# Causal mask of the query maxima added by VectorE, strip by strip, and the batches written out one by one

## What is computed

```python
def _L0_attn_ref(x, Wq, Wk, Wv, Wo):
    def proj(W):                       # 16 heads, 32 values each (real and imaginary part)
        return (x @ W).reshape(B, N, H, 2 * hd).transpose(0, 2, 1, 3)
    ...
    scores = (einsum(q_r, k_r) + einsum(q_i, k_i)) / sqrt(hd)
    scores = where(tril(ones((N, N))), scores, -inf)
    probs = softmax(scores, axis=-1)
    ...
    return out @ Wo
x = x + _L0_attn_ref(_layernorm(x), Wq, Wk, Wv, Wo)
x = x + _L0_xattn_ref(_layernorm(x), ctx, ctx)
x = x + _L0_ffn_ref(_layernorm(x), kernel, bias, a, b)
```

## Time and profile before

| | us |
|---|---|
| median of 3 runs | 828.6 (827.96 to 828.76) |
| the profiled execution | 827.51 |
| its span, first to last instruction | 825.7 |

### The profile page before, as it was taken

The page is one execution under the profiler, slowest core; times in us unless marked ns, Lnnn a source line. Parts: engine busy times, 40 slices in busy tenths (PEclk is TensorE's granted clock), DMA queues, the critical chain, the costliest instruction groups (busy, mean ns, idle before and its releaser), DMA issues.

```text
span 825.7 us, 15873 instructions
## 1 busy us (share of the span) xinstructions
PE 760.1 (92%) x5563; PEld 522.5 (63%) x5563; DVE 630.2 (76%) x1251; ACT 402.8 (49%) x760; POOL 472.1 (57%) x428
## 2 busy tenths in 40 slices
PE   3688999999999999999999999999999998989997
PEld 2565655765566556666666666565766564578995
DVE  2554555457769897999879997999788988798873
ACT  5114555555555466545645563647464546541111
POOL 5000000031966789677858786878677788975541
PEclk9759999999999999999999999999999998999997
DMA  5886656866686668566656675667466760101001
GB/s 180 111 105 83 98 78 85 135 83 85 84 135 78 90 85 135 74 89 108 90 101 89 103 93 100 89 104 96 71 95 109 95 88 8 58 14 36 5 13 38
DMA packets 47979, 70.53 MB, mean 85 GB/s; under 512 B 4897, under 2 KB 22578, under 8 KB 47922
## 3 DMA queue, kind: packets, MB, share of 16 engines
q1 hardware_dynamic: 46898, 69.52, 56.1%
q10 hardware_dynamic: 1024, 0.26, 0.1%
HBM read 14.98 MB, written 4.19 MB: 23 GB/s over the span
## 4 chain that ended last, share of the span: by engine, by line
PE 61%; DVE 15%; DMA 15%; issue 4%; ACT 2%; POOL 1%; SPq 1%; DVEq 0%; ACTq 0%; POOLq 0%
PE misc L521 21%; PE exp_bank L521 15%; DMA stack_k<-k_lo 14%; PE acc_bank L521 10%; PE max_bank L521 10%; PE sum_bank L521 3%; DVE neg_max L1205 3%; DVE score_rows L1217 2%; DVE head_out L1217 2%; SPq L452 1%; DVE seg_max L1205 1%; DVE ln_raw L1183 1%; PE misc L565 1%; ACT max_row L883 1%; PE misc L632 1%
## 5 line engine op out<-in xcount | busy, mean ns | idle before, releaser
L930 ACT ACTIVATE probs<-exp_bank 128x512 f32<-128x512 f32 x320 | 188.4, 592 | 203.7 <-PE exp_bank L521 200.9
L1205 DVE TENSOR_REDUCE neg_max<-max_bank 128x1 f32<-128x512 f32 (+1 forms) x192 | 130.3, 683 | 92.0 <-PE max_bank L521 91.5
L1580 POOL TENSOR_TENSOR prod<-head_probs,ctx_sb 128x256 f32<-128x256 f32 (+1 forms) x100 | 185.0, 1882 | 2.2 <-POOL head_probs L1575 0.5
L521 PE MATMUL max_bank<-stack_k,stack_q 96*128 96x384 f32 (+3 forms) x512 | 158.2, 372 | 17.1 <-DMA stack_k<-k_lo 8.7
L521 PE MATMUL acc_bank<-probs,values 128*32 128x512 f32 (+3 forms) x1024 | 158.6, 447 | 4.3 <-ACT log_sum L941 2.3
L314 POOL TENSOR_TENSOR prod<-x1n,ctx_sb 128x256 f32<-128x256 f32 (+1 forms) x104 | 158.7, 1557 | 4.3 <-ACT x1n L890 4.3
L521 PE MATMUL sum_bank<-probs,ones 128*32 128x512 f32 (+3 forms) x1024 | 157.8, 444 | 0.0
L521 PE MATMUL exp_bank<-stack_q,stack_k 97*128 97x384 f32 (+3 forms) x512 | 149.9, 355 | 1.8 <-DVE wf_lo L1175 1.3
L521 PEld LDWEIGHTS exp_bank<-stack_q,stack_k 97*128 97x128 f32 x512 | 84.5, 195 | 56.8 <-issue 26.5
L1520 POOL TENSOR_TENSOR ln_var<-ln_mv,eps 128x4 f32<-128x4 f32 x21 | 4.4, 210 | 197.8 <-DVE ln_mv L1191 197.8
L1205 DVE TENSOR_REDUCE seg_max<-max_bank 128x4 f32<-128x512 f32 x128 | 87.1, 683 | 29.2 <-PE max_bank L521 27.7
(11 more groups left out here) (181 smaller groups left out, 1381.8 us busy)
## 6 DMA issues: line engine op xcount, KB each, us to landing
stack_q<-q_hi SPq DMA_DIRECT2D x64, 256.0 KB, 5.6
stack_k<-k_hi SPq DMA_DIRECT2D x64, 256.0 KB, 9.5
stack_q<-q_lo SPq DMA_DIRECT2D x32, 256.0 KB, 7.0
stack_k<-k_lo SPq DMA_DIRECT2D x32, 256.0 KB, 10.7
x_in<-in_x SPq DMA_DIRECT2D x9, 512.0 KB, 5.5
ctx_sb<-in_ctx SPq DMA_DIRECT2D x32, 128.0 KB, 3.2
x<-in_x SPq DMA_DIRECT2D x7, 512.0 KB, 10.1
out<-y_sb SPq DMA_DIRECT2D x5, 512.0 KB, 3.3
```

Source lines behind the costliest of these rows:

```text
L521: return nc.tensor.matmul(*args, **kw)
L930: nc.scalar.activation(probs[:, (UNITS * g + n) % PTR, :], exp_bank[n % 2][:, :], ACT.Exp, scale=SCALE).then_inc(exp_done, 1)
L1205: vec.tensor_reduce(o, v, axis=AX_X, op=ALU.max, negate=True).then_inc(max_taken, 1)
L1580: last = gp.tensor_tensor(pv_prod[:, COFF[j]:COFF[j + 1]].rearrange("p (q d k) -> p q d k", q=4, k=keys), head_probs[:, 4 * j:4 * j + 4, N ...
```

## The change

It removes the mask matmul of every query unit, the tiles `mask_q`, `seg_max` and `neg_max`, the semaphore `max_ready` and the two small instructions behind the tenth unit. `take_max` issues one `tensor_tensor_reduce` per block instead, 16 per group in place of 10 reduces: it adds the right-hand end of `causal` (bf16, 512 columns, zero but for the last 128) to the block in place in PSUM, and keeps the maximum. Each of these is two instructions on DVE, the sum and a read of the accumulator, both shown as `ISA`. Its wait carries a wait on `const_ready` (long past) ahead. PE turns the maxima when `max_taken` has counted all ten units, and ACT negates them as it copies. The key side keeps its mask. The loop over batches is gone: all batches are written out.

```diff
     def batches(self, eng, body, n_batch):
-        first, after = 3, n_batch - 2
-        for i in range(-1, first):
-            body(i, i)
...
-        for i in range(after, n_batch):
+        for i in range(-1, n_batch):
             body(i, i)
...
-            def scores(bank, unit, lhs, rhs, slot, rows, key_side, done):
+            def query_scores(bank, unit, slot):
+
+                for h, blk, at, width in unit[0]:
+                    last = mm(bank[:, at:at + width], stack_q[0:STACK, slot, h, blk * P:(blk + 1) * P],
+                              stack_k[0:STACK, slot, h, 0:width], start=True, stop=True, skip_group_check=True)
+                last.then_inc(max_scored, 1)
...
             def turn_maxima(slot):
-                pe.wait_ge(max_ready, n_max_ready.up())
+                pe.wait_ge(max_taken, n_max_ready.up(UNITS))
...
-                            copy(max_row[:, m_slot % 2, :], misc[0][0:G * NT, 0:P]).then_inc(max_row_ready, 1)
+                            nc.scalar.activation(max_row[:, m_slot % 2, :], misc[0][0:G * NT, 0:P], ACT.Identity,
+                                                 scale=-1.0).then_inc(max_row_ready, 1)
...
             def take_max(n, ring):
 
-                dve.wait_ge(max_scored, n_scored.up())
+                wait_apart(dve, const_ready, (max_scored, n_scored.up()))
                 bank = max_bank[n % 2]
-                if n < G:
-                    o, v = neg_max[:, ring, n:n + 1, 3], bank[:, :]
-                elif n < 2 * G:
-                    o, v = seg_max[:, n - G, :], bank[:, :].rearrange("p (s k) -> p s k", k=P)
-                else:
-                    h = 2 * (n - 2 * G)
-                    o, v = neg_max[:, ring, h:h + 2, 1], bank[:, :].rearrange("p (s k) -> p s k", k=2 * P)
-                vec.tensor_reduce(o, v, axis=AX_X, op=ALU.max, negate=True).then_inc(max_taken, 1)
+                for h, blk, at, width in QUERY_UNITS[n][0]:
+                    v = bank[:, at:at + width]
+                    last = vec.tensor_tensor_reduce(v, v, causal[:, T - width:T], 1.0, -3.0e38, ALU.add, ALU.max,
+                                                    query_max[:, ring, h, blk:blk + 1])
+                last.then_inc(max_taken, 1)
...
-                            if unit == UNITS - 1:
-
-                                dve.wait_ge(max_taken, n_scored.now())
-                                vec.tensor_reduce(neg_max[:, ring, :, 2], seg_max[:, :, 0:3], axis=AX_X, op=ALU.min)
-                                vec.tensor_copy(neg_max[:, ring, :, 0], seg_max[:, :, 3]).then_inc(max_ready, 1)
```

More of the change, by code:

```diff
@@ L233, in decoder_layer @@
         stacked, max_stacked = sem("stacked"), sem("max_stacked")
-        max_scored, max_taken, max_ready = sem("max_scored"), sem("max_taken"), sem("max_ready")
+        max_scored, max_taken = sem("max_scored"), sem("max_taken")
         max_psum, max_row_ready = sem("max_psum"), sem("max_row_ready")
@@ L502, in _ @@
             n_stack, n_row = turn.count(16 * STACK_DMAS * NG), turn.count(16 * NG)
-            n_max_bank, n_max_ready = turn.count(UNITS * NG), turn.count(NG)
+            n_max_bank, n_max_ready = turn.count(UNITS * NG), turn.count(UNITS * NG)
             n_exp_bank, n_probs, n_v = turn.count(UNITS * NG), turn.count(UNITS * NG), turn.count(NG)
@@ L590, in project_v, with key_scores @@
                 last.then_inc(v_psum, 1)
-            def scores(bank, unit, lhs, rhs, slot, rows, key_side, done):
+            def query_scores(bank, unit, slot):
[3 more added lines that the diff above has]
+                last.then_inc(max_scored, 1)
+            def key_scores(bank, unit, slot):
                 parts, (col, count, step) = unit
                 for n, (h, blk, at, width) in enumerate(parts):
-                    first = blk * P if key_side else 0
-                    mm(bank[:, at:at + width], lhs[0:rows, slot, h, blk * P:(blk + 1) * P],
-                       rhs[0:rows, slot, h, first:first + width], start=(n == 0), stop=False,
+                    mm(bank[:, at:at + width], stack_k[0:STACK + 1, slot, h, blk * P:(blk + 1) * P],
+                       stack_q[0:STACK + 1, slot, h, blk * P:blk * P + width], start=(n == 0), stop=False,
                        skip_group_check=True)
-                mask = mask_k if key_side else mask_q
                 if count == 1:
-                    o, m = bank[:, col:col + P], mask[:, :]
+                    o, m = bank[:, col:col + P], mask_k[:, :]
                 else:
                     o = bank[:, :].rearrange("p (a n) -> p a n", n=P)[:, col // P:col // P + step // P + 1:step // P, :]
-                    m = mask[:, None, :].to_broadcast([P, 2, P])
-                mm(o, ident_b[:, :], m, start=False, stop=True, skip_group_check=True).then_inc(done, 1)
+                    m = mask_k[:, None, :].to_broadcast([P, 2, P])
+                mm(o, ident_b[:, :], m, start=False, stop=True, skip_group_check=True).then_inc(exp_scored, 1)
             def attend(units, slot, first_tile):
@@ L1528, in _ @@
             gp.memset(ident[:, :], 0.0)
-            gp.memset(mask_q[:, :], 0.0)
+            gp.memset(causal[:, :], 0.0)
             gp.memset(mask_k[:, :], 0.0)
```

15 lines of the change are left out of this document (6 added, 9 removed).

## The result

The changed kernel takes 823.7 us against 827.5, medians of 16 runs of each: 0.9943 of the time before, 95% interval 0.9927 to 0.996. The profiled execution took 824.57 us with a span of 822.8, against 827.51 and 825.7. Several of its terms did not come out so, and the larger misses cancelled. Most of what follows is about them.

What follows compares the result with a forecast made beforehand. PE (92% busy), DVE and the stack's transfers were taken to bound the kernel in turn. Terms -2.2 - 2.4 + 2.5 - 0.3 - 0.7 - 0.7 - 0.3 = -4.1 us, from 828.6 to 824.5; range 812 to 850.

Steps and rivals of the forecast that it cites:

- The floor: Stack transfers plus the serial 4.7 us from landing to next issue: no stage of four heads under about 18.9 us.
- The prediction's own sign against itself: Prediction is wrong if DVE idles in batch 4, g = 2, meaning PE or the transfers still lead there.
- PE, 1.1 us per group: Removing ten mask matmuls per group saves PE 1.1 us, 35 us over 32 groups if PE were the only limit.
- DVE, +0.9 us per group: 16 sums with reads replace 10 reduces and two small instructions: 7.5 us against 6.6; bounds -0.2 to +2.8.
- rival 3: DVE's sum in PSUM runs at half rate or is blocked by POOL: about +100 us, 930; chance 0.06.
- g = 0 and g = 1: g = 0: -1.1 each in batches 0 and 1, then -0.4; g = 1: -0.1 each in batches 0 to 2, then +0.5.
- g = 2, -0.7: Stages g = 2: -0.2 each in batches 3 to 6, +0.3 in batch 2, -0.1 each in the first two.
- g = 3, -0.7: Stages g = 3: DVE stays under the transfer limit, one mask leaves the serial 4.7 us: -0.1 each.
- The loop, -0.3: Writing out all batches saves 0.3 us for the loop's registers, with bounds 0 and 2.
- Slope of 325 us per microsecond of block: Kernel time per extra DVE time per block; 0.013 us more per block would eat the whole gain.
- rival 2: The read or sum on DVE costs more, 0.12 us per block: +35 us, 863; chance 0.27.
- Rival 1: The read hides beside the next block, DVE's work falls 0.2 us, PE's gain arrives: -17 us, 811.5; chance 0.15.

Runs made afterwards that it cites:

- the one with DVE's gap at the loop: The changed kernel with batches 3, 4 and 5 run again in one loop on the engines; 833.3 us (1.0063).
- the last: The changed kernel with xt_lo and x2t_lo first (811.0 us), its accumulation of units 8 and 9 moved behind the projection of q on PE; 836.4 us (1.0114).

## Why the prediction came out right

**What bounds the kernel.** The floor holds: (4,3) takes 18.8 to 19.2 us in nine of the eleven kernels of the experiments (not in the one with DVE's gap at the loop, and not in the last), whether PE has 1.1 us less or DVE 1.1 more, and the early stages of the last one show that PE's part is in it. That PE and DVE both fill (4,2) holds in part: 2 us less on DVE alone gave 0.6 us, the move of the mask alone 1.4, both 1.7. The prediction's own sign against itself came: DVE idles 0.8 us in (4,2), and PE leads there.

**PE, 1.1 us per group.** Too high, about 0.8. A unit with its mask and the same unit without, first the kernel before, then the changed one:

```profile
457.04 0.48 PE L521 MATMUL max_bank<-stack_k,stack_q 96*128 96x384 f32 x2
457.36 0.28 PE L521 MATMUL max_bank<-mask_q,ident_b 128*128 128x256 bf16 x1
457.40 0.36 PE L521 MATMUL misc<-wf_hi,x2t_hi 128*128 128x256 f32 x1
...
459.19 0.48 PE L521 MATMUL max_bank<-stack_k,stack_q 96*128 96x256 f32 x2
459.52 0.28 PE L521 MATMUL max_bank<-mask_q,ident_b 128*128 128x256 bf16 x1
459.73 0.52 PE L521 MATMUL acc_bank<-probs,values 128*32 128x384 f32 x2
```

```profile
452.55 0.49 PE L508 MATMUL max_bank<-stack_k,stack_q 96*128 96x384 f32 x2
452.87 0.33 PE L508 MATMUL misc<-wf_hi,x2t_hi 128*128 128x256 f32 x1
...
454.63 0.49 PE L508 MATMUL max_bank<-stack_k,stack_q 96*128 96x256 f32 x2
455.05 0.52 PE L508 MATMUL acc_bank<-probs,values 128*32 128x384 f32 x2
```

The unit takes 0.32 us and not the 0.24 of the projection that the prediction set beside it. Its mask costs 0.04 (0.36 against 0.32) where scores or a projection follow, and 0.12 (0.54 against 0.42) where an accumulation follows, 0.08 there if the mask has 128 columns. By the medians of these cases that is 0.8 us per group, 25 in all. Busy time fell by 1.3 us in (4,2), 1.1 in (1,0), 0.8 in (4,3) and 0.6 in (5,1).

**DVE, +0.9 us per group.** Mis-sized. The read costs 0 to 0.05 us and not 0.07, and DVE grows by 0.2; the busy time rose by 6.5 us, where about 30 was forecast. The lower bound (read hidden) was the better value. The sum on an operand in PSUM in place costs as a reduce does, so rival 3 is out. No POOL contention on it: right.

**g = 0 and g = 1.** The mechanism, the low parts behind longer units on DVE, was right, and g = 1 without the clock is +1.3 where +2.0 was forecast. In g = 0 the wait for `xt_lo` (0.73 to 0.82 us) ate nearly all of it: -0.4 and not -2.0. What was left out is that PE's gain turns into idle time ahead of the same wait, and that the clock can fall behind idle time: 1.55 us each in (4,1) and (6,1). The prediction has no term for the clock behind batch 0.

**g = 2, -0.7.** The step that failed worst: measured -7.2. The forecast kept DVE's 20.60 us of work in (4,2), added 0.9 and took DVE for the limit, so that PE's gain counted for nothing. But the move of the mask alone, with the sum still held, is worth 1.4 of the 1.7 us: PE led. And 1.9 us of DVE's work was one sum held by a product, a matter of 0.2 us in time, and it went away, worth another 0.3. The earlier trace rows had shown the mean of 915 ns; the single values were not read.

**g = 3, -0.7.** Without the low clock about -1.0 in all, so of the right size. But PE's waits at unit 0 for the stack did not grow (0.37, 0.26 and 0.33 us in (3,3) to (5,3), against 0.58, 0.36 and 0.32).

**The loop, -0.3.** Right for the kernel before, by windows inside and outside. Wrong for this change: with the loop the mask change is 0.6% slower than the kernel before. The two parts of the change were added as if they were independent, and writing the batches out was worth 9.6 us.

**Slope of 325 us per microsecond of block.** Six times too steep; it took every stage as led by DVE. So rival 2 was dangerous only from about 0.07 us per block (an estimate, the gain of 4.1 over the slope), and its 0.27 was too much. Rival 1's 811.5 was a fair price for PE's share (813.3), but its condition alone did not suffice. The terms that it lists add up to about -16 rather than -17.

So that the number 824.5 was met is luck: a gain missed in g = 2 (6.5 us) stood against the low clock, g = 0 and the end. The sign rested on PE's gain against a small cost on DVE, and for the written-out kernel that holds. With the loop it would have been wrong, and the prediction gave no reason that tells the two apart.

## What to carry to other kernels

Moving work off the busiest engine pays only as far as the next wait of that engine lets it; look at what stands in the other engine's queue ahead of the result that it waits for, and move that too (here eight lines moved, 12.7 us by the medians). A mean over instructions of one line hides collisions: read least and most before a stage's work is taken as fixed. Parts of a change that look independent (a longer instruction stream, a loop) should be priced together.

## What the runs showed of the hardware

- `tensor_tensor_reduce` on 512 columns, in place in PSUM with a bf16 operand in SBUF, takes 0.62 us start to start with its accumulator read; the read adds 0 to 0.05.
- A DVE sum of two SBUF operands that starts 0.2 us behind a GpSimd product was held until about its end (2.33 us for 0.4); one that started just ahead took 0.39, and the product 2.45 for 2.22.
- The granted clock fell to 0.5 for 3.4 us behind an idle 1.39 us of PE, in two of four equal places (in 5 of 16 over four kernels), and stayed up there when the gap was filled with useless matmuls. Each such stretch cost 1.55 us.
- A mask matmul of 256 bf16 columns, recorded at 0.28 us, moved what follows by 0.04 us ahead of scores or a projection and by 0.12 ahead of an accumulation.
- A jump back in DVE's stream cost 2.7 us of idle time with the longer body, with instruction transfers in the gap; the shorter body had neither.
